# Reordering the first stage of a fused attention kernel and splitting its first loads over two queues

## What is computed

```python
q = x @ Wq                                   # x is layer-normed
k, v = jnp.split(context @ Wkv, 2, axis=-1)
k = concatenate((null_key, k)); v = concatenate((null_value, v))
q = jnp.tanh(q); k = jnp.tanh(k)
attn = softmax(einsum('bhid,bhjd->bhij', q, k) * 64 ** -0.5)
out = einsum('bhij,bhjd->bhid', attn, v)     # then @ Wout + bout
```

## Time and profile before

| | us |
|---|---|
| median of 3 runs (lowest, highest) | 215.52 (214.39, 215.72) |
| the profiled execution: time | 214.31 |
| its span in the profile | 212.5 |
| PE, DVE, ACT, POOL busy | 195.8, 146.0, 120.6, 39.1 |

### The profile page before, as it was taken

How to read it: one execution, slowest core, us unless ns; L and a number is a source line. 1 busy time by engine, 2 the same in 40 slices (tenths; PEclk the granted TensorE clock), 3 DMA queues, 4 the chain that set the end, 5 groups by cost and what they waited for, 6 DMA issues and landing times.

```text
span 212.5 us, 4137 instructions
## 1 busy us (share of the span) xinstructions
PE 195.8 (92%) x1627; PEld 146.2 (69%) x1629; DVE 146.0 (69%) x249; ACT 120.6 (57%) x221; POOL 39.1 (18%) x40
## 2 busy tenths in 40 slices
PE   6895679999999999999999999999988899999991
PEld 1793578898988889888988877956755334635560
DVE  3459798889788799998988869833873737124313
ACT  3197678788888888878888864004631123331300
POOL 4139202204022040220311700020401400000001
PEclk9999999999999999999999999999999999999999
DMA  5896669971102011010000695999999400000000
GB/s 170 286 390 173 144 191 349 369 199 51 52 2 97 3 49 52 0 52 0 2 3 0 232 386 176 324 382 377 378 377 377 160 0 0 3 0 0 3 0 28
DMA packets 22853, 31.02 MB, mean 146 GB/s; under 512 B 1953, under 2 KB 18866, under 8 KB 22834
## 3 DMA queue, kind: packets, MB, share of 16 engines
q1 hardware_dynamic: 22834, 30.76, 43.2%
HBM read 29.57 MB, written 0.13 MB: 140 GB/s over the span
## 4 chain that ended last, share of the span: by engine, by line
PE 53%; issue 21%; DVE 13%; ACT 4%; DMA 3%; POOL 2%; SPq 1%; POOLq 0%; DVEq 0%
PE ps L1008 34%; PE ps L1042 6%; DVE keys L734 5%; DMA w_k_stage<-in_Wkv 3%; PE ps L1082 2%; PE ps L1096 2%; DVE ex_l L700 2%; PE ps L1188 1%; DVE mixT L744 1%; PE ps L996 1%; DVE q_split L725 1%; PE ps L1069 1%; PE ps L1172 1%; PE ps L1227 1%; DVE ex_sum L755 1%
## 5 line engine op out<-in xcount | busy, mean ns | idle before, releaser
L734 DVE SCALAR_TENSOR_TENSOR keys<-ps,keys 64x512 f16<-64x512 f32 x64 | 44.1, 689 | 7.1 <-ACT keys L573 5.7
L1008 PE MATMUL ps<-ctxT_h,w_k_h 128*128 128x256 f32 x128 | 39.4, 308 | 2.5 <-DVE keys L734 2.1
L573 ACT ACTIVATE keys<-ps 64x512 f16<-64x512 f32 x64 | 37.8, 591 | 1.8
L1008 PE MATMUL ps<-ctxT_h,w_k_l 128*128 128x256 f32 x128 | 36.6, 286 | 0.0
L1008 PE MATMUL ps<-ctxT_l,w_k_h 128*128 128x256 f32 x128 | 36.6, 286 | 0.0
L1008 PEld LDWEIGHTS ps<-ctxT_h,w_k_h 128*128 128x128 f32 x128 | 24.8, 194 | 4.2 <-issue 3.0
L569 ACT ACTIVATE ps<-ps 128x512 f32<-128x512 f32 x32 | 18.6, 582 | 14.7 <-PE ps L1008 14.7
L700 DVE TENSOR_TENSOR ex_l<-ps,ex_h 128x512 fp32r<-128x512 f32 x32 | 22.1, 691 | 6.7 <-ACT ps L603 6.1
L1008 PE MATMUL ps<-ex_h,ctx_h 128*128 128x512 f32 x64 | 25.7, 401 | 0.0
L1008 PE MATMUL ps<-ex_l,ctx_h 128*128 128x512 f32 x64 | 25.3, 395 | 0.0
L1008 PEld LDWEIGHTS ps<-ctxT_l,w_k_h 128*128 128x128 f32 x128 | 25.0, 195 | 0.0
(11 more groups left out here) (175 smaller groups left out, 260.2 us busy)
## 6 DMA issues: line engine op xcount, KB each, us to landing
w<-in_fc1T SPq DMA_DIRECT2D x8, 1024.0 KB, 12.3
w<-in_fc SPq DMA_DIRECT2D x8, 1024.0 KB, 11.9
stage_t<-in_ctxT SPq DMA_DIRECT2D x8, 256.0 KB, 5.0
stage_n<-in_ctx SPq DMA_DIRECT2D x8, 256.0 KB, 4.6
w_k_stage<-in_Wkv SPq DMA_DIRECT2D x4, 256.0 KB, 6.2
mixT<-in_Wq SPq DMA_DIRECT2D x2, 512.0 KB, 6.2
q_two<-q_split SPq DMA_DIRECT2D x8, 128.0 KB, 4.0
w_v<-in_Wkv SPq DMA_DIRECT2D x1, 1024.0 KB, 5.4
```

The lines of the kernel that those rows point to most:

```text
L573: nc.scalar.activation(keys[rows, u % 2, PK * i:PK * (i + 1), r], full[rows].rearrange("p (j n) -> p j n", j=PK), ACT.Copy, scale=UNIT).th ...
L734: V.scalar_tensor_tensor(out=keys[other, u % 2, PK * i:PK * (i + 1), r], in0=ps[mine, K_BANK + kp % 2].rearrange("p (j n) -> p j n", j=PK) ...
L1008: last = MM(dst, lhs[i], rhs[j], start=start and m == 0, stop=stop and m == len(parts) - 1)
```

## The change

On SP the two spreads move ahead of the rest of `const` and the small vectors, and ctxT 2 and ctx 2 ahead of them too. ACT issues eight of the first loads itself: ctxT 0, key weights 0 to 2, the second half of Wq, key weights 3, ctx 0, ctxT 1. PE projects the first half of the queries before any key, the second half after key projection 2; the null scores follow scores 0 and 1. All four low parts of key weights are POOL's, the high parts of pieces 2 and 3 are DVE's. POOL clears `ex_sum` at the start; null sums of sequence 1 are copied in during step 2 or later, those of sequence 0 are added after its steps. `high_ctxT(n+2)` moves from block 4n+3 to block 4n+1. The rest of SP's order (eight bias rows, w_v, w_out, second-block weights, then ctxT 3) stays.

```diff
-        NULL_BANK = (3, 0)
+        NULL_BANK = (0, 3)
...
             sp.dma_start(x0[:], a["x"]).then_inc(ld_x, 16)
+            sp.dma_start(w_q_half(w_q, 0), w_q_half(chunked("Wq"), 0)).then_inc(ld_wq[0], 16)
             sp.dma_start(const[:, 0:C_STRICT], a["const"][:, 0:C_STRICT]).then_inc(ld_eye, 16)
-            load_wk(0)
-            load_ctxT(0)
-            for half in range(2):
-                cols = slice(half * 512, (half + 1) * 512)
-                sp.dma_start(w_q[:, :, cols], chunked("Wq")[:, :, cols]).then_inc(ld_wq[half], 16)
-            load_wk(1)
             sp.dma_start(null_k[:], a["null_k"]).then_inc(ld_null, 16)
             sp.dma_start(null_v[:], a["null_v"]).then_inc(ld_null_v, 16)
-            load_wk(2)
-            load_wk(3)
-            load_ctx(0)
-            load_ctxT(1)
+            spread_queries(0)
             load_ctx(1)
+            spread_queries(1)
+            load_ctxT(2)
+            load_ctx(2)
             sp.dma_start(const[:, C_STRICT:], a["const"][:, C_STRICT:]).then_inc(ld_const, 16)
...
             sp.dma_start(b1[:], a["b1"]).then_inc(ld_small, 16)
...
-            spread_queries(0)
-            spread_queries(1)
...
             sp.dma_start(w_v[:], a["Wkv"][:, INNER:2 * INNER].rearrange("(c p) n -> p c n", p=P)).then_inc(ld_wv, 16)
             sp.dma_start(w_out[:], chunked("Wout")).then_inc(ld_wv, 16)
-            load_ctxT(2)
-            load_ctx(2)
             sp.dma_start(w_lq[:], chunked("lWq")).then_inc(ld_lin, 16)
...
+            nc.gpsimd.memset(ex_sum[:], 0.0).then_inc(zero_ready, 1)
...
-                pool.wait_ge(wk_high, i + 1)
+                if i < 2:
+                    pool.wait_ge(wk_high, i + 1)
+                else:
+                    pool.wait_ge(wk_later, i - 1)
                 low_part(w_k_piece(w_k_l, i), w_k_piece(w_k_stage, i), w_k_piece(w_k_h, i)).then_inc(wk_ready[i], 1)
...
+            def null_rows(b, r):
+                row = slice(64 * r, 64 * r + 1)
+                sums = ex_sum[row].rearrange("p (j r) b q -> p r b j q", r=2)[:, r, b]
+                return sums, null_ex[row].rearrange("p j (b q) -> p b j q", b=B)[:, b]
...
                 if n == 0:
-                    nc.gpsimd.memset(ex_sum[:], 0.0).then_inc(zero_ready, 1)
-                    low_wk(2)
-                    low_wk(3)
+                    for i in range(G * KT):
+                        low_wk(i)
                     low_ctxT(1)
-                    pool.wait_ge(zero_ready, 1)
-                    pool.wait_ge(ctxT_ready, 1)
-                    pool.wait_ge(null_ready, 2)
-                    for r in range(2):
-                        row = slice(64 * r, 64 * r + 1)
-                        heads = ex_sum[row].rearrange("p (j r) b q -> p r j (b q)", r=2)[:, r]
-                        nc.gpsimd.tensor_copy(heads, null_ex[row]).then_inc(null_sums, 1)
-                    pool.wait_ge(null_sums, 2)
                     low_ctx(0)
-                    for n in range(1, B * NC):
-                        low_ctx(n)
-                        if n + 1 < B * NC:
-                            low_ctxT(n + 1)
+                    for i in range(1, NC):
+                        low_ctx(i)
+                        low_ctxT(i + 1)
+                        if i == 1:
+                            pool.wait_ge(zero_ready, 1)
+                            pool.wait_ge(null_ready, 2)
+                            pool.wait_ge(ctxT_ready, i + 1)
+                            for r in range(2):
+                                sums, mine = null_rows(1, r)
+                                nc.gpsimd.tensor_copy(sums, mine).then_inc(null_sums, 1)
+                            pool.wait_ge(null_sums, 2)
+                    for i in range(NC, B * NC):
+                        low_ctx(i)
+                        if i + 1 < B * NC:
+                            low_ctxT(i + 1)
+                        if i == NC:
+                            pool.wait_ge(esum_ready, STEPS // B)
+                            pool.wait_ge(ctxT_ready, i + 1)
+                            for r in range(2):
+                                sums, mine = null_rows(0, r)
+                                nc.gpsimd.tensor_tensor(sums, sums, mine, ALU.add).then_inc(null_sums, 1)
+                            pool.wait_ge(null_sums, 4)
...
+            def queries_tanh(g):
+                act.wait_ge(q_psum, g + 1)
+                nc.scalar.activation(qT[:, PG * g:PG * (g + 1)], ps[:, 1 + g].rearrange("p (j t) -> p j t", t=P),
+                                     ACT.Tanh).then_inc(q_tanh, 1)
+            def null_exp(g):
+                act.wait_ge(null_psum, g + 1)
+                nc.scalar.activation(null_ex[:, PG * g:PG * (g + 1)], ps[:, NULL_BANK[g]].rearrange("p (j t) -> p j t", t=P),
+                                     ACT.Exp, scale=DH ** -0.5).then_inc(null_ready, 1)
+            def load_wk(i):
+                act.dma_start(w_k_piece(w_k_stage, i), w_k_source(i)).then_inc(ld_wk[i], 16)
+            act.dma_start(stage_t[:, 0], ctxT_source(0)).then_inc(ld_ctxT[0], 16)
+            load_wk(0)
+            load_wk(1)
+            load_wk(2)
+            act.dma_start(w_q_half(w_q, 1), w_q_half(chunked("Wq"), 1)).then_inc(ld_wq[1], 16)
+            load_wk(3)
+            act.dma_start(stage_n[:, 0], ctx_source(0)).then_inc(ld_ctx[0], 16)
+            act.dma_start(stage_t[:, 1], ctxT_source(1)).then_inc(ld_ctxT[1], 16)
             split_wk(0)
-            act.wait_ge(ld_ctxT[0], 16)
-            copy(ctxT_h[:, 0], stage_t[:, 0], first_high)
             split_wk(1)
+            queries_tanh(0)
+            keys_tanh(0)
+            keys_tanh(1)
             act.wait_ge(ld_null, 16)
             nc.scalar.activation(null_kt[:], null_k[:], ACT.Tanh).then_inc(nk_tanh, 1)
-            keys_tanh(0)
-            for j in range(2):
-                act.wait_ge(q_psum, j + 1)
-                src = ps[:, 1 + j].rearrange("p (j t) -> p j t", t=P)
-                nc.scalar.activation(qT[:, 4 * j:4 * j + 4], src, ACT.Tanh).then_inc(q_tanh, 1)
-                split_wk(2 + j)
-            keys_tanh(1)
-            for j in range(2):
-                act.wait_ge(null_psum, j + 1)
-                nc.scalar.activation(null_ex[:, 4 * j:4 * j + 4], ps[:, NULL_BANK[j]].rearrange("p (j t) -> p j t", t=P),
-                                     ACT.Exp, scale=DH ** -0.5).then_inc(null_ready, 1)
             keys_tanh(2)
+            queries_tanh(1)
...
                 nc.scalar.activation(full, full, ACT.Exp, scale=SCORE_SCALE).then_inc(e_ready, 1)
+                if s < G:
+                    null_exp(s)
                 if s + AHEAD < STEPS:
                     keys_tanh(s + AHEAD)
...
-            def split_wk(i):
-                dve.wait_ge(wk_high, i + 1)
-                low_part(w_k_piece(w_k_l, i), w_k_piece(w_k_stage, i), w_k_piece(w_k_h, i)).then_inc(wk_ready[i], 1)
+            def high_wk(i):
+                dve.wait_ge(ld_wk[i], 16)
+                V.tensor_copy(w_k_piece(w_k_h, i), w_k_piece(w_k_stage, i)).then_inc(wk_later, 1)
...
                 if s == 0:
-                    dve.wait_ge(null_sums, 2)
+                    dve.wait_ge(zero_ready, 1)
                 else:
                     dve.wait_ge(esum_ready, s)
+                if s == STEPS // B:
+                    dve.wait_ge(null_sums, 2)
                 V.tensor_tensor(total, total, ps[:, S_BANK + s % 2].rearrange("p (h q) -> p h q", q=S),
                                 ALU.add).then_inc(esum_ready, 1)
             dve.wait_ge(ld_x, 16)
             norm_stats(0, x0[:])
+            dve.wait_ge(ld_ctxT[0], 16)
+            V.tensor_copy(ctxT_h[:, 0], stage_t[:, 0]).then_inc(first_high, 1)
             normalise(0, xn[:], x0[:]).then_inc(xn_ready, 1)
-            split_wk(0)
             dve.wait_ge(first_high, 1)
             low_part(ctxT_l[:, 0], stage_t[:, 0], ctxT_h[:, 0]).then_inc(first_ready, 1)
             dve.wait_ge(xnT_psum, 1)
             V.tensor_copy(xnT[:], ps[:, 0, 0:DC * P].rearrange("p (c t) -> p c t", c=DC)).then_inc(xnT_ready, 1)
-            split_wk(1)
+            high_wk(2)
             split_queries(0)
+            high_wk(3)
+            low_keys(0)
+            low_keys(1)
             high_ctxT(1)
-            low_keys(0)
+            high_ctx(0)
+            low_keys(2)
             split_queries(1)
-            low_keys(1)
-            high_ctx(0)
...
                 if s >= 1:
                     add_to_sum(s)
-                if s == 0:
-                    low_keys(2)
                 if s + AHEAD < STEPS:
                     low_keys(s + AHEAD)
                 n = b * NC + c
                 if t == 0 and g == G - 1 and n + 1 < B * NC:
                     high_ctx(n + 1)
-                if t == KT - 1 and g == G - 1 and n + 2 < B * NC:
+                if t == KT - 1 and g == 0 and n + 2 < B * NC:
                     high_ctxT(n + 2)
```

(109 more changed lines are left out.)

## The result

The changed kernel takes 223.42 us (median; 222.53 to 223.73) against 215.62 before: ratio 1.0329, 95% interval 1.0284 to 1.0375. The two medians divide to 1.036; the ratio is estimated from the undisturbed executions alone, and one of the four before, of 487.87 us, is not among them. The kernel is slower, as forecast; the forecast was 220.7, and the range 216.5 to 223.5 held the median by less than 0.1. The profiled execution took 223.73 us, with a span of 221.5 against 212.5. The profile of the kernel before, with 214.31 us, is of a shorter execution than any other of that kernel on record (214.39 to 218.94, the 487.87 aside), so differences between the two profiles come out larger than between the medians.

What follows compares the result with a forecast made beforehand. PE alone was taken to bound the kernel after 28.7 us, with DVE's moved wait for ctxT 3 opening a hole: 4.65 - 0.6 + 1.7 = 5.75 on 214.31 gives 220.1, with half of 1.2 added 220.7 us; range 216.5 to 223.5.

Steps and rivals of the forecast that it cites:

- The sum of 5.75: Whole kernel: 4.65 lost at scores(9), 0.6 gained at the middle gap, 1.7 lost to slow clock; 5.75 us slower.
- Unit matrix and `q_low`: First stage: unit matrix there at 7.3 us, `q_low` reaching 2 at 22.3, with 20.5 and 24.5 as ends.
- the forecast gain of 1.2: End of first stage: scores(2) start at 27.5 rather than 28.73, 1.2 us gained, between 0 and 3.
- Landing of ctxT 3: SP's queue: the load DVE's moved cast waits for lands at 51.3 us, from 49.5 to 53.5.
- PE has scores(8) waiting for the sum and projection 11 for `low_keys(9)`: PE behind DVE's wait: projection 11 starts at L + 3.2, then 18 products take 2.9 before scores(9).
- L: Landing time of ctxT 3, 51.3; scores(9) forecast at L + 6.1 = 57.4 against 52.75 before, 4.65 us lost.
- Slow clock: Products behind PE's 4.9 us hole: run at 1.2 GHz rather than 2.4, 1.7 us lost, between 0 and 3.
- Middle gap: PE's idle gap at 94.22, waiting for `ctxT_l`: goes because `ctxT_h` is made two steps sooner, 0.6 us gained.
- rival 4: Wait for ctxT 3 hidden: break-even at landing 47.25, full gain below 45.4, kernel faster at 213.1 us; chance 0.09.
- Edits that cost nothing: Null copies, POOL's low parts of key weights, ACT's eight issues: no cost; ACT's first copy at about 6.3.
- Rival 2: First stage slower than thought: `q_low` at 24.5, ctxT 3 landing at 53.5, 2.2 us more loss, 222.9 us; chance 0.13.
- rival 3: ctxT 3 arrives about as before, 46.5 to 48; hole -0.2 to 1.3, 215.5 us, no change; chance 0.08.

Runs made afterwards that it cites:

- experiment 1: Changed kernel with the load of ctxT 3 issued right after ctxT 2 and ctx 2, ahead of constants and weights: 214.07 us, again 213.83.
- experiment 2: Changed kernel with high_ctxT(n+2) back at the end of block 4n+3: 217.87 us, ratio 1.0061.
- second trial: The changed kernel run again as it is, on the chip of another run: 224.00 us, ratio 1.0369.
- experiment 3: The kernel before with only high_ctxT moved to block 4n+1: 222.37 us, ratio 1.0270.
- experiment 5: Changed kernel with key projection 10 computed five times over (223.49 us, again 224.39) or seven times over (222.41 us).
- experiment 8: Changed kernel with ctxT 3 early, unit matrix first, null value late, plus more warming products on PE around the transposes: 211.54 us, ratio 0.9786.

## Why the prediction was right, and where it was off

The mechanism was the forecast one, in place and order: DVE in front of ctxT 3 (forecast 7 to 9 us, measured 10.21), projections behind it, slow products, the gap near 94 gone. Experiments 1 and 2 take the late load and the forward wait away one at a time: with the first all of the loss goes, with the second most of it (1.0061 is left). The sum of 5.75 came out as 9.0 on the span, and as 7.8 between the medians. That the range held the median is in part luck: the profiled execution, with 223.73, and the median of the second trial, with 224.00, lie beyond its end of 223.5. By terms:

- **Unit matrix and `q_low`.** Taken at 7.3, the matrix was there at 8.5, later than the 7.1 to 8 of equal sharing; `xnT` 0.9 to 1.0 later than the 8.7 of the forecast. The queries at the slow level were right (3.76 for 3.6). `q_low` 2 came at 23.65, not 22.3, and scores(2) at 28.52, released by the sum of step 0 and not by the spread: the forecast gain of 1.2 was 0.2 against this profile of the kernel before. The Trainium skill's rule (DMA: Bandwidth & Descriptors, "Issuing engines are not separate DMA queues") agrees with these rows: from 3 to 9 us traffic was 291 GB/s with one issuer and 285 with two, x landed 3.1 after its issue against 2.0 before, and putting the matrix first only moved the wait to Wq.
- **Landing of ctxT 3.** Forecast 51.3, measured 53.66. Of the 2.4, 1.35 are `q_low`'s, 0.4 a slower pace of SP between it and w_v (12.5 for 12.1), 0.6 the full stretch behind w_v (17.5 for 16.9).
- **The step of the argument that failed: "PE has scores(8) waiting for the sum and projection 11 for `low_keys(9)`".** Scores(8) need both keys of their unit, and the second is key 9. So scores too stand behind the keys, L + 3.2, and the step takes its whole 3.38 from there: scores(9) at L + 6.6, not L + 6.1. That is 0.5 of the loss. PE's hole before scores(8) was 8.1 us long and not 4.9: 1.5 of the difference is this step, 2.4 the later landing, less 0.7 by which the hole began later.
- **Slow clock.** 2.0 for 1.7.
- **Middle gap.** 0.6, as forecast: scores(9) are 9.6 later than before, the span 9.0 longer.
- **A wait read wrongly.** For rival 4 it was said that the wait for ctxT 2 in block 3 cost PE nothing. It cost 0.2 (experiment 3). It is in the 52.75 from which the sum counts, so the sum stays as it is.
- **Edits that cost nothing.** Null sums on POOL, its low parts of the key weights, ACT's issues: none shows in the chain. ACT's table load began at 6.42 and its first copy at 7.85, not 6.3, still ahead of PE's key projection 0 at 13.2.

Rival 2, the first stage slower than thought, came nearest in size (222.9), and about half of its mechanism held: the matrix was late and `q_low` 2 came between the forecast's 22.3 and the rival's 24.5. Rival 4 and rival 3 asked for the load at 45 to 48; experiment 1 shows that rival 4's mechanism was one line away.

## What to carry to other kernels

When a wait is moved forward on an in-order engine, look up when the thing waited for is issued and lands, and everything that the same change puts in front of it on its queue: here the consumer moved two steps up and the load seven microseconds down. Loads needed by date belong ahead of loads needed later in a queue; 4 MB of weights, of which PE reads the first at 140.9, stood before 256 KB that the next step wanted. A hole in PE can cost more than its length, by slow products behind it: 2.0 here behind 8.1 us, 1.6 in experiment 2 behind 2.51.

## What was not expected of the hardware

- The clock level behind a short hole is not the same from execution to execution. After 2.51 us of idle PE (experiment 2) and after 2.08 (experiment 5) the products ran at 1.2 GHz, in the second case only from 1.4 us after the restart; after 1.62 us in another execution of the same kernel, and after the idle stretch of 2.33 us in the first stage of the kernel before (the forecast had it as 2.5), they did not. Averages over the runs hide this.
- Sixteen query products took 3.76 and 3.45 us in the two profiles of the changed kernel, and 2.02 where PE was kept busy before them (experiment 8). The granted clock read 1.00 throughout the first stage of the changed kernel's first profile all the same; with the unit matrix first, where they took 3.75, it read 0.66 between 7 and 9 us.
